# A two-layer graph network on one core: the class comparison of layer 0 as seven one-tensor operations, and four index loads and one turn placed ahead of the x scatter's wait

## What is computed

```python
e_feat = concat([x[rol], x[col], edge_attr], -1)      # layer 0
v = relu(e_feat @ W1 + b1) @ W2 + b2
x0 = maximum(segment_max(v, col), x)
x = layernorm(x + x0)
xs, y = x[src], x[dst]                                # layer 1
msg = einsum('eb,ebo->eo', w_comp[etype], einsum('ei,bio->ebo', xs, weight))
a = tanh(relu(sum((xs @ A1.T + A1_b) * (y @ A2.T + A2_b + rel_emb[etype]), -1) / sqrt(32)))
nei = segment_sum(a[:, None] * msg, dst)
x = layernorm(x + relu(where(in_deg > 0, nei + x[src[last_e]] @ self_loop_weight, 0)))
```

## Time and profile before

| | us |
|---|---|
| median of 3 runs | 4698.58 (4695.10 to 4704.23) |
| the profiled execution's own time | 4697.75 |
| its span, first to last instruction | 4696.0 |
| PE busy | 3559.1 (76%) |
| POOL busy | 3502.1 (75%) |
| DVE busy | 2630.5 (56%) |
| layer 0's gathers on POOL, from step 8 on | 305.64 to 2101.66 |

### The profile page before, as it was taken

One profiled execution on the slowest core, in us unless ns is written; L12 is line 12 of the kernel. 1 busy time (PEld: TensorE's weight loads), 2 busy tenths in 40 slices (PEclk: granted clock), 3 DMA queues, 4 the chain that ended last, 5 costly groups with the idle time before them and its releaser, 6 DMA issues.

```text
span 4696.0 us, 62687 instructions
## 1 busy us (share of the span) xinstructions
PE 3559.1 (76%) x18080; PEld 1650.3 (35%) x18279; DVE 2630.5 (56%) x3543; ACT 924.9 (20%) x1615; POOL 3502.1 (75%) x3530
## 2 busy tenths in 40 slices
PE   5639999998999999981047777777777777777751
PEld 2315555544444444441013333233333333323321
DVE  5624444434434333434137777777777777777754
ACT  3401111111111111110012222222222222222211
POOL 7777777777777777767777777777777777777755
PEclk8869999999999999995568888988888888888875
DMA  8123333322222222223134454454454454445521
GB/s 312 28 58 79 79 75 78 78 71 69 69 71 68 67 70 70 69 55 64 33 91 121 126 121 119 124 125 115 123 125 120 118 124 126 119 121 125 120 67 33
DMA packets 387141, 448.88 MB, mean 96 GB/s; under 512 B 165171, under 2 KB 288976, under 8 KB 384752
## 3 DMA queue, kind: packets, MB, share of 16 engines
q1 hardware_dynamic: 241968, 197.51, 18.8%
q0 software_dynamic: 112832, 141.36, 13.0%
q10 hardware_dynamic: 32256, 109.07, 6.0%
HBM read 324.74 MB, written 122.85 MB: 95 GB/s over the span
## 4 chain that ended last, share of the span: by engine, by line
DMA 32%; issue 12%; POOL 5%; PE 1%; DVE 0%; POOLq 0%; ACT 0%; DVEq 0%; ACTq 0%
DMA xg<-h_dram,src_idx 30%; POOL xg L541 4%; DMA last_rows<-sum_rows,last_i 2%; DVE late L994 0%; PE psum L1193 0%; PE psum L1184 0%; POOL last_rows L541 0%; PE psum L1235 0%; POOLq L536 0%; DVE scan L1009 0%; DMA sum_rows<-early 0%; PE psum L1170 0%; PE psum L1242 0%; POOLq L362 0%; PE psum L1099 0%
## 5 line engine op out<-in xcount | busy, mean ns | idle before, releaser
L541 POOL DMA_INDIRECT xg<-h_dram,src_idx x1664 | 1603.6, 964 | 536.1 <-DMA xg<-h_dram,src_idx 471.1
L541 POOL DMA_INDIRECT xg<-in_x_dram,src_idx x1468 | 1514.6, 1032 | 457.8 <-DMA xg<-in_x_dram,src_idx 413.5
L994 DVE TENSOR_TENSOR late<-late,psum 128x512 f32<-128x512 f32 x1664 | 1107.0, 683 | 547.8 <-PE psum L1184 523.8
L1113 PE MATMUL psum<-late 128*128 128x448 bf16 x4116 | 862.1, 363 | 0.0
L1235 PE MATMUL psum<-ident,xg 128*128 128x128 f32 x1664 | 332.2, 336 | 462.9 <-DMA xg<-h_dram,src_idx 455.5
L1184 PE MATMUL psum<-comp,sel 128*128 128x512 bf16 x1482 | 590.9, 419 | 8.6 <-DVE late L994 4.0
L1113 PEld LDWEIGHTS psum<-late 128*128 128x128 bf16 x4116 | 411.3, 101 | 465.2 <-issue 154.8
L922 DVE TENSOR_TENSOR_SCAN scan<-fresh,scan,psum 128x512 f32<-128x512 bf16 x103 | 131.8, 1280 | 762.8 <-PE psum L1151 762.8
L1193 PE MATMUL psum<-late,basis 128*32 128x512 f32 x3328 | 515.2, 696 | 4.3 <-DVE late L994 0.8
L1235 PEld LDWEIGHTS psum<-ident,xg 128*128 128x128 f32 x1664 | 259.9, 176 | 535.0 <-issue 471.2
L686 ACT COPY late<-psum 128x512 f32<-128x512 f32 x416 | 243.9, 586 | 853.4 <-PE psum L1235 806.5
(11 more groups left out here) (137 smaller groups left out, 3505.9 us busy)
## 6 DMA issues: line engine op xcount, KB each, us to landing
sp_in<-spread SPq DMA_DIRECT2D x208, 256.0 KB
late<-type_dram SPq DMA_DIRECT2D x104, 512.0 KB, 8.4
sum_rows<-early ACTq DMA_DIRECT2D x104, 512.0 KB
spread<-late ACTq DMA_DIRECT2D x16, 1664.0 KB, 38.2
ea<-in_edge_t SPq DMA_DIRECT2D x104, 256.0 KB, 2.7
keep<-keep_dram SPq DMA_DIRECT2D x832, 32.0 KB
max_rows<-out ACTq DMA_DIRECT2D x104, 256.0 KB, 2.0
xg<-h_dram,src_idx POOLq DMA_INDIRECT x1664
```

Source lines behind the costliest of these rows:

```text
L541: pool.indirect_dma_start(out=out, out_offset=None, in_=table, in_offset=bass.IndirectOffsetOnAxis(ap=index, axis=0), engine_sem=pool_issu ...
L994: dve.tensor_tensor(prod[:, n % G_BUFS, :], x4[:, s.slot(2), g, :], bank[C_BANK[n]][:, :], ALU.mult).then_inc(prod_ready, 1)
L1113: last_ = pe.matmul(bank[8 - HOT + tile][:, 0:PICK * F], class_hot[:, s.slot(2), c, P * tile:P * tile + P], x_parts[:, c, q, :], start=c = ...
```

## The change

There are three edits.

1. **`build_hot`.** One `tensor_tensor` over 128 x 1792 elements, whose two inputs are both broadcast views in SBUF (the class numbers and the seven class values), becomes seven `tensor_scalar` over 128 x 256 elements. Each of them reads the 256 class numbers and takes its class value as one scalar for each partition. The last of the seven signals `hot_built`.
2. **SP.** A new constant `AHEAD = 4`: the indices of steps 8 to 11 are loaded behind the wait for `class_out` and ahead of that for `x_spread`; `loads0` leaves them out, in its steps 2 to 5.
3. **PE.** The turn of the gathered rows of step 0 is called ahead of the loop (`source_turn0`), behind a wait for `dve_counted` (the search has let go of the PSUM bank that the turn writes) and ahead of the wait for `parted` (constants in bf16 parts).

```diff
+AHEAD = 4
@@ sync
             sp.wait_ge(class_out, 16)
+            for n in range(PRE, PRE + AHEAD):
+                index_load0(Step(PRE, n // PRE, n % PRE))
             sp.wait_ge(x_spread, 16 * NODE_COLS)
...
-                if index.exists() and (not s.known or index.at >= PRE):
+                if index.exists() and (not s.known or index.at >= PRE + AHEAD):
                     index_load0(index)
@@ vector, build_hot
-                size = [P, CLASSES, HOT * P]
-                dve.tensor_tensor(class_hot[:, u, :, :], bc(class_in[:, u, :], size, 1),
-                                  bc(class_id[:, :], size, 2), ALU.is_equal).then_inc(hot_built, 1)
+                for c in range(CLASSES):
+                    last_ = dve.tensor_scalar(class_hot[:, u, c, :], class_in[:, u, :], class_id[:, c:c + 1], None,
+                                              ALU.is_equal)
+                last_.then_inc(hot_built, 1)
@@ tensor
             pe.wait_ge(loaded, 16 * N_CONST)
-            pe.wait_ge(parted, 1)
...
-            def step0(s):
-                u = s.slot(2)
+            def source_turn0(s):
+
                 wait_count(pe, s, gathered[0][s.slot(PRE)], gathered0(s, 1))
...
                 last_.then_inc(x_turned[0], 1)
+
+            def step0(s):
+                u = s.slot(2)
+                if not s.known or s.at > 0:
+                    source_turn0(s)
                 wait_step(pe, s, d_ready[0], lag=1)
...
+            pe.wait_ge(dve_counted, 2 * (NODE_COLS // 2 + 1))
+            source_turn0(Step(PRE, 0, 0))
+            pe.wait_ge(parted, 1)
             run_steps(pe, step0, PRE)
```

## The result

The changed kernel takes **4573.73 us** (median, 4571.65 to 4578.58) against 4701.40 us for the kernel before on the same chip: ratio 0.9724, 95% interval 0.9707 to 0.9740. The prediction was 4586 us with a range of 4568 to 4630. The profiled execution has a span of 4570.7 us, and the gain lies where the sum had put it, in POOL's gathers of layer 0.

A forecast was written before the change was run, and what follows sets the result against it. POOL's gathers were taken to bound layer 0. Removing the comparison holds (-118.3 us), the new operations' price (+14.7) and the earlier start (-8.6) sum to -112.2 us, giving 4586 us, range 4568 to 4630.

The forecast's parts named there:

- POOL as the bound, and the sum over its row: Layer 0's end is POOL's start plus 1343 gather intervals and their stretching; later stages move as a block.
- The 118.3 us of edit 1: POOL's gathers in layer 0: removing 98 long comparison holds of 1.21 us each saves 118.3 us.
- undisturbed intervals: Spacing of POOL's gathers in layer 0 without stretching: 1.248 us each, 1676.1 us for 1343.
- The price of the new operations: Delay to POOL's gathers from the seven-operation trains: 0.15 us a step, 14.7 us; bounds 0 to 34 us.
- the model: A gather's request beside a DVE train waits at most for one operation's rest, 0 to 0.2 us, on average 0.1.
- The Trainium skill's rule: In the new trains a gather would be stopped twice at 0.1 us: 23.5 us in all, time 4595 us.
- Edit 2: Start of POOL's step 8: with indices there, the first gather moves from 305.64 to 297.01, saving 8.6 us.
- The cover of 1.1 us for step 9: Step 1's turn is done at 313.35 and POOL comes to step 9 at 314.5, leaving 1.1 us to spare.
- Edit 3: PE's turn of step 0 some 13 us earlier lies wholly under PE's 82.37 us wait: 0 us.
- The rival of the unopened train: POOL gets in only after all seven comparison operations, losing 0.7 us a train, 68.6 us: 4640 us; chance 0.09.
- the eleven pairs: Eleven traced pairs of DVE operations without a wait where POOL got in at the boundary; evidence against an unopened train.
- PE as the bound: Late in layer 0 PE needs 17.1 to 18 us a step, giving back 11 us: 4597 us; chance 0.06.

The follow-up runs named there:

- e2: Changed kernel with the one tensor_tensor comparison back, keeping the early index loads and early turn; 4695.07 us, ratio 0.9975.
- e1: Kernel before with only the new build_hot (seven tensor_scalar), index loads and turn as before; 4592.64 us, ratio 0.9761.
- e5: Changed kernel with the seven tensor_scalar comparing with constants instead of one class value per partition (wrong rows, measuring only); 4589.05 us, ratio 0.976.
- e6: Changed kernel with each of the seven tensor_scalar writing 128 elements instead of 256 (wrong rows, measuring only); 4581.70 us, ratio 0.9744.
- e4: Changed kernel with seven two-input tensor_tensor of 128x256 in place of the seven tensor_scalar; 4609.08 us, ratio 0.9801.
- e10: Changed kernel run again as it is, on one chip with the variant keeping layer 1's weighted messages in PSUM; 4578.36 us, ratio 0.9728.
- e11: Changed kernel with layer 1's weighted messages kept in PSUM, so the running sum reads one SBUF tensor, second run; 4558.06 us, ratio 0.9693.
- e7: Changed kernel with one tensor_scalar over 128x1792 in place of the seven (wrong rows, measuring only); 4580.27 us, ratio 0.9736.
- e3: Changed kernel with step 0 turned behind the wait for parted again, the other two edits kept; 4582.43 us, ratio 0.9746.

## Why the prediction was right, point by point

**POOL as the bound, and the sum over its row: right.** The last gather of layer 0 moved from 2100.72 to 1978.07, by 122.7 us, and the profiled span by 125.3. What lies behind the last gather took 2595.3 us before and 2592.6 after.

**The 118.3 us of edit 1: right.** Beyond the undisturbed intervals there were 119.0 us and there are 4.4. e2 has 120.2 with the old comparison and e1 has 6.1 with the new one, so it is this operation and none of the other edits.

**The price of the new operations: mis-sized.** This is the term that failed, though within its bounds of 0 to 34 us. 14.7 us were taken (0.15 us for each train); the 98 trains cost 0.6 us. All else beyond the undisturbed intervals was put at 0.7 us (118.3 of 119.0 before) and measures 3.8, of which the wait in step 9 has 1.3. Together that is 15.4 us expected and 4.4 measured, and these 11.0 are most of the 12.3 us by which the forecast lay above the measured time. Two readings went into the term. The length was too short: 0.34 us each and 0.263 apart, not 0.29 and 0.20. And the model, that a request waits for the rest of the running operation, was taken from the operation L908 (L912 now). It about holds for the quicker operations of e5 and e6 (0.07 and 0.05 us a request) and does not for these. Here DVE gives way instead. In every one of the 98 trains one or two operations last up to 0.55 us in place of 0.34, and the one behind starts about 1.0 us after the start of a gather. The trains are 2.05 to 2.39 us long, where seven unpushed operations would take 6 x 0.263 + 0.34 = 1.92 us. By the model the longer train would have made the term larger. So the term erred twice, in opposite directions. (A price of 0, the lower bound, gives 4571 us and not the 4568 of the range; the measured time lies inside either way.)

**The Trainium skill's rule** ("SBUF — State Buffer", section "Who interferes with whom") gave 23.5 us for this term, since both a gather's reads and its writes were to wait. For the kernel as changed the trace disagrees: 0.6 us in the trains, and it is DVE that waits. Its part on two SBUF inputs agrees with e4 (24.1 us in the trains) and with the running sum in e10 and e11 (32 us and none). Its statement that an operation with at most one SBUF input, outside the two-port modes, doesn't contend fits e7, which runs at the slow rate and stretches nothing. The product of e11, with one SBUF input, 0.69 us for 512 elements and 10.4 us of stretch, does not fit it. Its part on a one-input operation that holds up writes too is seen in e5 alone, if that is what a gather's later part is.

**Edit 2: right in its main term, with one wait put at nothing.** 8.6 us expected. The idle time went from 8.93 to 0.30 us, e2 alone gives 9.3 us, and e3 against e1 10.2. The cover of 1.1 us for step 9 was a misreading: it took the moment at which POOL's engine comes to step 9 (314.5 in the forecast), while POOL's queue asks 2.8 us before that moment, and the turn comes in between. On POOL's row e2 gains 7.3 us over the kernel before, not 8.6.

**Edit 3: right**, 0 us by e3.

**The rival of the unopened train: real, but not here.** It was priced for every train. e4 and e5 each show it in 6 trains of 98 (in e5 for the later part of a gather), and the changed kernel in none. That the eleven pairs of the kernel before spoke against it was right for those pairs, and no proof for a train of seven.

**PE as the bound: fell.** PE's pace beyond its waits is 16.4 us late in layer 0 (17.51 a step between the turns of steps 83 and 102, less 1.14 of wait), not 17.1. With waits of 1.0 to 1.2 us ahead of every turn the granted clock stayed at 1.00; with waits of up to 3.4 us, as before, it was 0.96. PE met POOL at step 82, not 75, because POOL was quicker than forecast.

## What to carry to other kernels

An engine that only issues transfers by index can be the bound at 75% busy. Its row has to be read for the spacing of the issues and for single ones that are longer than the rest, and their ends compared with the ends of what runs on the vector engine. Where they agree to 0.01 us, the first thing to change is the number of tensors that the vector operation reads out of SBUF, not its speed: a slower form that reads one, or reads the second from PSUM, can be worth more than a faster one that holds the other engine up. The quicker one-tensor form of e5 lost 14 us against the slower one, so each form has to be measured. An earlier start of the bounding engine adds to the gain, less what it then runs into: here 1.3 of 8.6 us went to a wait that its queue reaches 2.8 us before its engine does.

## What the runs showed of the hardware

- A gather by index asks for something 0.13 us after its start. If a vector operation with two SBUF tensors is running, it waits until that ends, and is done 0.81 us later (2.02 us operation, gathers of up to 2.81 us), or 0.75 us in layer 1 (1.28 us operation).
- One `tensor_scalar` over 1792 elements with a value for each partition (2.06 us, 1.12 ns an element, broadcast input) holds up no gather. Dense ones of 256 elements run at 0.52 ns an element.
- A `tensor_tensor` with one input in SBUF and one in PSUM (512 elements) held up 40 gathers of e11 by 10.4 us in all, and the same operation in e10 by 0.4 us; the reason is open.
- A `tensor_scalar` with a value for each partition costs 0.06 us more than with a constant (starts 0.263 and 0.202 us apart at 256 elements).
- Beside such dense operations with a value for each partition the gathers are not held (0.6 us over 98 trains of seven), and DVE is: one operation in a train lasts up to 0.55 us in place of 0.34. With constants (starts 0.202 us apart) a request waits 0.07 us on average.
- POOL's queue comes to a step's condition 2.8 us before the step's first gather starts (all 13 profiled executions). Where it was held there for 1.70 us, POOL later had 1.64 us of idle time.
- Back-to-back operations can shut POOL out for the whole of a train: 6 of 98 trains, up to 1.78 us, both for two-input operations and, in a gather's later part, for quick one-input operations with constants. A semaphore wait between them removed this for the two-input ones.
- The part behind layer 0, which is the same code, took 2592.6 us in one profiled execution of the changed kernel and 2603.4 in the other (4570.7 - 1978.1 and 4581.5 - 1978.1). The busy time of layer 1's gathers differs by 10.9 us between the two. So the difference of some 11 us is in those gathers. Stretched gathers beside the running sum have 22 us in the one and 32 in the other; what sets how the two fall together is open.
